# A hybrid attention, state-space and mixture block on one core: passes, sums and a root put at other places

## The chip, the cores and the metric

The kernel runs on one NeuronCore of a Trainium2 chip. TensorE (PE) multiplies, VectorE (DVE), ScalarE (ACT) and GpSimd (POOL) work element by element, and SyncE (SP) issues the transfers. The metric is the device time in microseconds from start to end of one execution. Each engine takes its own instructions strictly in the order in which the program gives them; between engines only semaphores order the work (`wait_ge` holds an engine until a counter is reached, `then_inc` counts up when an instruction is done).

## The reference, cut to what matters

Input is x, 2 batches of 1024 tokens with 128 features, in 32-bit floats. Four blocks follow each other, each on a layer norm of x and each added to x:

```
x = x + attention(layernorm(x))     # 16 heads of 64, causal, values = keys
x = x + ffn(layernorm(x))           # 16 experts of width 64, the best two of 16, and a shared one
x = x + state_space(layernorm(x))   # convolution, gated scan over the tokens
x = x + ffn(layernorm(x))           # the same weights again
```

Attention computes softmax(q k^T / 8) k for each head, masked above the diagonal. Its denominators are sums of exponentials over the keys. The mixture computes for each token `silu(x wg) * (x wu)` for every expert, weights it by the router's share (zero for all but two), and multiplies by wd; it adds the result to the normed input and to x.

## The kernel before, in words

**Attention** (function `attention`, lines 242 to 880) works through 16 units. A unit is a pair of heads (l = 0, 1) of one batch: 1024 queries against 1024 keys, cut by causality into 9 slots of at most 512 query columns for both heads. A slot is a segment of scores for a key block j and query blocks a to b. TensorE fills a pair of PSUM banks with a slot's scores (`scores`, `mask`), ScalarE takes the exponential into SBUF (`exponentials`, L525, one instruction of 128 x 1024 for both heads), TensorE multiplies the keys by it (`outputs`, L783) in five bursts r = 0 to 4. The outputs of a unit run one unit later, beside the next unit's scores; unit 15, the last, has its outputs behind all scores, alone. GpSimd adds the exponentials over the key blocks (`add_up`, L427, 11 sums n = 0 to 10 for each unit; sums 4 to 10 are for the second half of the queries). TensorE then makes a total over partitions (`denominators`, L797), ScalarE the reciprocal (Ln, Exp: L516, L518), and VectorE scales the outputs by it (`scale_out`, L613). The outputs of the first half of a unit's queries lie in the bank `out_ps`, and those of the second half too, except in the last unit, where they lie in a bank of the ring. So outputs of unit 15 may not start before unit 14's second half has been scaled out of `out_ps`:

```
if r == 0:
    pe.wait_ge(knat_done, g + 1)
    wait(pe, out_used, 2 * g)      # g = 15: the 30th scale_out, unit 14, second half
```

VectorE's own order in a unit is: scale the unit before, first half (r = 0), maxima for the unit after, and at r = 4 scale the unit before, second half. In unit 15 there are no maxima to take. GpSimd's wait for a sum is on the exponentials it reads (`exp_done`) and on the sum before.

**The prologue of attention** (L815 to L838) sets up the first two units: TensorE turns the normed input, projects keys and queries, fills banks with scores from which VectorE takes the row maxima (`max_scores(0, m)`, L716; `maxima`, L583 and L587; m = 0 to 9), projects unit 1 (`project`, L680 to L682, 12 passes of 512 columns), turns its keys (`turn_keys(1)`), turns the maxima (`turn_max(0)`, L726) and makes five idle multiplications (`warm`, L808, 128 x 128 in 32-bit floats, two records each in the trace). `warm` exists to keep TensorE at work. The banks of the ring are reused in the written order `PROLOGUE`: m = 8 waits until m = 6 has been read.

**The mixtures** (`mixture`, twice: tags m1 and m2) go through 4 groups of 512 tokens, 9 steps each (8 pairs of experts and the shared one). A step g on TensorE is six passes of 512 columns (`up`, L1047 to L1049: three into a bank g_ps, three into a bank u_ps, both in rings of two) and, two steps later, the down product (`down`, L1058, eight instructions). Between them lie silu on ScalarE (L1142), the weighting on GpSimd (L1280: needs the weights wb, which SyncE spreads by DMA from a tensor in memory), and the product with u_ps on VectorE (L1196, `hid`). A u_ps bank is free for step g when hid of step g - 2 is done. Around the steps, each engine emits the preparation of the groups (source, statistics, root, norm, turn, high and low part, logits, route, turned weights `turn_w`) at due times written out by hand (`PREPARE`, `OWN`, `SOURCE_TILES`): a piece with due time -5 comes before one with -4.5, all with due times below 0 ahead of step 0. In the second mixture the group 0 comes normed from the state-space stage (`first`, early = 1), and the sources of groups 1 to 3 go to g_ps[1], u_ps[0] and u_ps[1].

Of the kernel before, what the change touches and what calls it, by code (L numbers as in the profile page):

```python
# [237 lines left out]
def attention(nc, k, w_qk, x_view, load_w_out):  # L238
# [5 lines left out]
    with Scope(nc, "at") as s:  # L244
# [34 lines left out]
        scores_ready, exp_done, av_done, summed = s.sem("scores_ready"), s.sem("exp_done"), s.sem("av_done"), s.sem("summed_up")  # L279
        den_ready, ln_done, inv_done, out_used = s.sem("den_ready"), s.sem("ln_done"), s.sem("inv_done"), s.sem("out_used")  # L280
        inv_spread = [s.sem(f"inv_spread{h}") for h in range(2)]

# [101 lines left out]
        with nc.Block() as block:  # L384
# [31 lines left out]
            def _(pool):  # L416
                def add_up(unit, n):
# [6 lines left out]
                    wait(pool, summed, NSUM * unit + n)  # L424

                    def add(a, b, left, right):
                        return pool.tensor_tensor(sums[:, :, a * P:b * P], left, right, ALU.add)  # L427

# [139 lines left out]
            def _(dve):  # L568
# [36 lines left out]
                def scale_out(g, half):  # L605
# [3 lines left out]
                    else:  # L609
# [4 lines left out]
                       .then_inc(out_used, 1)  # L614

                clear(dve)
                for n in range(EARLY):
# [24 lines left out]
                for unit in range(UNITS):  # L642
                    more = unit + 1 < UNITS
                    for r, row in rounds(unit):
# [9 lines left out]
                        if r == 0 and unit and more:  # L654
                            keys_low(dve, unit + 1)
                        if r == NBURST - 1:
                            if more:
                                join_maxima(unit + 1)
                            if unit:
                                scale_out(unit - 1, 1)  # L660
                            if more:
                                max_rows(unit + 1)
                            if unit + 2 < UNITS:
                                queries_low(unit + 2)
# [4 lines left out]
            def _(pe):  # L669
# [119 lines left out]
                def denominators(g, half):  # L789

                    pe.wait_ge(summed, NSUM * g + HALF_SUMS[half])
                    if half:
                        pe.wait_ge(rows_done, min(g + 2, UNITS))
# [34 lines left out]
                norm.turn(pe, EARLY + 1)  # L828
                for m in (6, 7, 8):
                    max_scores(0, m)  # L830
                pe.wait_ge(norm.low, GROUPS)
                max_scores(0, 9)
                project(1, "K")
                project(1, "Q")
                turn_keys(1)
                turn_max(0)
                warm(5, out_ps)
# [53 lines left out]
       1: dict(norm=-5.8, residual=-6, turn=-4.5, high=-4, low=-4, natural=1.5, route1=1.6),  # L891
       2: dict(statistics=-4.2, root=-4.1)}
ORDER = ["source", "add_up", "sigmoid"] + [p for p in PREPARE if p != "sigmoid"]


def agenda(pieces, with_finish, tiles=False):

    found = []
    for n in range(GROUPS):
        for piece in pieces:  # L900
# [3 lines left out]
            if piece in PREPARE:  # L904
                at = PREPARE[piece] + STEPS * n
                if piece == "root" and n == 1:
                    at = PREPARE["sigmoid"]
                at = OWN.get(n, {}).get(piece, at)
                found.append((at, piece, n, "prepare"))
# [55 lines left out]
def mixture(nc, tag, k, f, source, source_ready=None, load_x=None, weights=None, next_norm=False, store=None, ahead_of=None, first=None):  # L965
# [9 lines left out]
    with Scope(nc, tag) as s:  # L975
# [12 lines left out]
        before, after = first or GroupNorm(s, "before"), GroupNorm(s, "after") if next_norm else None  # L988
        early = 1 if first else 0

        own = s.ps("own")
# [48 lines left out]
        with nc.Block() as block:  # L1040
            @block.tensor
            def _(pe):
# [20 lines left out]
                def step(g):  # L1063
# [15 lines left out]
                    if g >= RING and (g - RING) % STEPS == LAST:  # L1079
                        pe.wait_ge(hid_ready, g - RING + 1)  # L1080
                    up(g_ps[r], f.wg_hi, f.wg_lo, st, n).then_inc(g_ready, 1)
                    if st < LAST:
                        wait(pe, hid_ready, g - RING + 1)
                        up(u_ps[r], f.wu_hi, f.wu_lo, st, n).then_inc(u_ready, 1)
# [6 lines left out]
                def emit(piece, n, kind):  # L1091
# [27 lines left out]
                    elif piece == "natural":  # L1119
# [6 lines left out]
                        last.then_inc(nat_ready, 1)  # L1126
                    elif piece == "turn_w":
                        pe.wait_ge(w_ready, n + 1)
                        for t in range(PER):
# [767 lines left out]
```

## Time and profile before

| what | us |
|---|---|
| median of the runs (730.75 to 732.27) | 731.11 |
| the profiled execution | 732.0 |
| its span, first to last instruction | 730.1 |
| TensorE busy | 707.1 (97%) |
| VectorE / ScalarE / GpSimd busy | 434.8 / 366.3 / 417.5 |
| mean granted clock of TensorE | 0.989 |

The profiled execution is 0.9 us above the median, and 1.9 us of it lie outside its span. In the page TensorE is at nine tenths or more in nearly all of the 40 slices; it is lower in the first and near 630 us. Its clock is at 0.6 in the second slice (18 to 36 us), and at 0.9 to 1.0 elsewhere. Attention ends at about 452.7 us, the first mixture begins at 453.0, the state-space stage at about 574 and the second mixture at about 626.

### The profile page before, as it was taken

The page shows a single profiled execution, that of the slowest core. Times are in us where ns is not written, and L with a number is a line of the kernel's source. Part 1 is how long each engine was busy: PE and PEld are TensorE (multiplying, and loading weights), DVE is VectorE, ACT ScalarE, POOL GpSimd, SP SyncE. Part 2 cuts the span into 40 slices and gives each one's busy share as a digit, 9 for nine tenths or more (in the row PEclk, how much of TensorE's full clock was granted, in tenths as well). Part 3 has the DMA queues.
Part 4 walks back from the last instruction along what each step waited for, and adds up shares of the span by engine and source line. Part 5 has one row for each costly group of instructions (what it writes and reads, how often), then busy time and mean ns, then how long its engine had stood idle before and what let it go on. Part 6 is the DMA issues. An engine that isn't in the chain of part 4 may idle for free. (4 is left out here: it accounts for less than half of the span.)

```text
span 730.1 us, 14977 instructions
## 1 busy us (share of the span) xinstructions
PE 707.1 (97%) x5675; PEld 499.7 (68%) x5675; DVE 434.8 (60%) x1214; ACT 366.3 (50%) x474; POOL 417.5 (57%) x310
## 2 busy tenths in 40 slices
PE   7899999999999999999999998999999999899998
PEld 6665665666566666566566655988888865678887
DVE  6776766765775775676676511455654657755433
ACT  4465554655555555555465542354664343555421
POOL 4486686677568659659657765144544422354543
PEclk9699999999999999999999999999999999999999
DMA  2000001001001001100100111723223000043332
GB/s 72 8 16 23 26 21 28 24 17 30 24 15 30 23 19 27 29 17 23 27 17 17 31 44 29 177 89 112 97 77 109 1 0 1 6 142 103 105 103 72
DMA packets 41276, 33.49 MB, mean 46 GB/s; under 512 B 14002, under 2 KB 32756, under 8 KB 41204
## 3 DMA queue, kind: packets, MB, share of 16 engines
q1 hardware_dynamic: 41204, 32.52, 15.4%
q8 instruction: 46, 0.75, 0.4%
q14 instruction: 26, 0.21, 0.1%
HBM read 23.32 MB, written 1.31 MB: 34 GB/s over the span
## 5 line engine op out<-in xcount | busy, mean ns | idle before, releaser
L427 POOL TENSOR_TENSOR all_x<-all_x,at_probs 128x1024 f32<-128x1024 f32 (+3 forms) x128 | 208.2, 1627 | 19.0 <-ACT at_probs L525 0.4
L525 ACT ACTIVATE at_probs<-at_ring 128x1024 f32<-128x1024 f32 x144 | 144.3, 1026 | 99.9 <-PE at_ring L762 98.7
L587 DVE CUSTOM_DVE_ANT_0 at_ring<-at_ring,at_after_query 128x128 f32<-128x128 f32 (+3 forms) x252 | 116.9, 516 | 69.1 <-PE at_ring L716 69.1
L783 PE MATMUL at_both<-at_probs,at_k_nat 128*64 128x512 f32 (+1 forms) x736 | 134.3, 493 | 0.2 <-issue 0.2
L1280 POOL TENSOR_TENSOR m_prod<-m_gate,m_wb 128x512 f32<-128x512 f32 x64 | 81.6, 1280 | 87.5 <-ACT m_gate L1142 79.8
L427 POOL TENSOR_TENSOR all_x<-at_probs 128x768 f32<-128x768 f32 (+1 forms) x32 | 67.3, 2102 | 105.1 <-ACT at_probs L525 102.4
L583 DVE TENSOR_REDUCE at_half_max<-at_ring 128x2 f32<-128x1024 f32 x64 | 78.3, 1225 | 42.6 <-PE at_ring L716 42.6
L783 PEld LDWEIGHTS at_both<-at_probs,at_k_nat 128*64 128x64 f32 x736 | 47.0, 136 | 65.3 <-issue 54.5
L1196 DVE TENSOR_TENSOR m_hid<-m_prod,m_u 128x512 f32<-128x512 f32 x64 | 43.7, 686 | 73.5 <-POOL m_prod L1280 70.0
L1058 PEld LDWEIGHTS m_acc<-rest_wd,m_hid 128*128 128x128 f32 (+1 forms) x576 | 74.4, 191 | 7.8 <-DVE m_hid L1196 2.2
L1142 ACT ACTIVATE m_gate<-m_g 128x512 f32<-128x512 f32 (+1 forms) x72 | 42.6, 597 | 70.1 <-PE m_g L1049 68.8
L1058 PE MATMUL m_acc<-rest_wd,m_hid 128*128 128x128 f32 (+1 forms) x576 | 76.1, 276 | 0.0
L716 PE MATMUL at_ring<-at_kh,at_qh 64*128 64x512 f32 (+2 forms) x380 | 71.4, 400 | 2.5 <-DVE at_half_max L583 1.5
L759 PE MATMUL at_ring<-at_qh,at_kl 64*128 64x512 f32 (+3 forms) x384 | 67.1, 343 | 0.0
L753 PE MATMUL at_ring<-at_qh,at_kh 64*128 64x512 f32 (+3 forms) x384 | 66.9, 344 | 0.1
L762 PE MATMUL at_ring<-at_m_rows,at_ones_r 64*128 64x512 f32 (+3 forms) x384 | 66.7, 342 | 0.0
L756 PE MATMUL at_ring<-at_ql,at_kh 64*128 64x512 f32 (+3 forms) x384 | 66.7, 342 | 0.0
L716 PEld LDWEIGHTS at_ring<-at_kh,at_qh 64*128 64x128 f32 x380 | 34.8, 189 | 29.1 <-issue 27.6
L753 PEld LDWEIGHTS at_ring<-at_qh,at_kh 64*128 64x128 f32 x384 | 36.6, 185 | 4.6 <-ACT at_probs L525 0.8
L759 PEld LDWEIGHTS at_ring<-at_qh,at_kl 64*128 64x128 f32 x384 | 36.5, 185 | 4.1
L762 PEld LDWEIGHTS at_ring<-at_m_rows,at_ones_r 64*128 64x128 f32 x384 | 36.6, 185 | 3.8
L756 PEld LDWEIGHTS at_ring<-at_ql,at_kh 64*128 64x128 f32 x384 | 36.3, 185 | 3.8
(254 smaller groups left out, 1189.6 us busy)
## 6 DMA issues: line engine op xcount, KB each, us to landing
m_wb<-m_wt_far SPq DMA_DIRECT2D x128, 128.0 KB, 2.9
at_inv<-at_inv_q SPq DMA_DIRECT2D x240, 32.0 KB, 1.9
all_x<-in_L_attn_a_x SPq DMA_DIRECT2D x8, 256.0 KB, 3.8
at_w_raw<-in_L_attn_a_W_qk SPq DMA_DIRECT2D x8, 128.0 KB, 2.5
out<-all_x SPq DMA_DIRECT2D x4, 256.0 KB, 2.4
a_room<-in_L_attn_a_W_out SPq DMA_DIRECT2D x1, 512.0 KB, 4.2
m_raw_wg<-in_L_ffn_experts_wg SPq DMA_DIRECT2D x1, 512.0 KB, 3.8
m_raw_wu<-in_L_ffn_experts_wu SPq DMA_DIRECT2D x1, 512.0 KB, 3.9
```

Source lines behind the costliest of these rows:

```text
L427: return pool.tensor_tensor(sums[:, :, a * P:b * P], left, right, ALU.add)
L525: act.activation(probs[:, :, slot * BANK:(slot + 1) * BANK], pair("S", unit, slot)[:, :, :], ACT.Exp, scale=BETA).then_inc(exp_done, 1)
L583: last = dve.reduce_max(half_max[:, :, i, out], pair("M", unit, m)[:, :, at:at + w], AX.X)
L587: last = dve.tensor_tensor_reduce(out=sums_ps, in0=sums_ps, in1=after_query[:, BANK - w:BANK], scale=1.0, scalar=MASKED, op0=ALU.add, op1= ...
L716: last = pe.matmul(out[:, l, at:at + (b - a) * P], qh[u][rows(l), i * P:(i + 1) * P], kh[u][rows(l), a * P:b * P], start=True, stop=True)
L753: pe.matmul(to[l], kh[u][rows(l), keys], qh[u][rows(l), q], start=first, stop=False, skip_group_check=True)
L756: pe.matmul(to[l], kh[u][rows(l), keys], ql[u][rows(l), q], start=False, stop=False, skip_group_check=True)
L759: pe.matmul(to[l], kl[u][rows(l), keys], qh[u][rows(l), q], start=False, stop=False, skip_group_check=True)
L762: last = pe.matmul(to[l], ones_r[rows(l), :], m_rows[u][rows(l), q], start=False, stop=True, skip_group_check=True)
L783: last = pe.matmul(out_bank(g, int(r > 0))[rows(l), o:o + (b - a) * P], k_nat[g % 3][:, j, rows(l)], probs[:, l, at:at + (b - a) * P], sta ...
L1058: last = pe.matmul(acc[:, t * P:(t + 1) * P], hid[g % BUFS][h, t * P:(t + 1) * P], f.wd[h, st, :], start=(st == 0 and t == 0), stop=(st == ...
L1280: pool.tensor_tensor(prod[g % BUFS][:, :], gate[g % BUFS][:, :], wb[q % SPREAD][:, :], ALU.mult)\
```

## The change

Four edits.

1. In unit 15 the sums 4 to 10 on GpSimd take head 0 alone (`heads`), and VectorE makes the same sums for head 1 (`last_sums`): the first four at r = 3, the last three at r = 4. The denominators of the second half wait for both.
2. In the prologue TensorE makes eight idle multiplications ahead of `max_scores(0, 8)`, into the bank that the projection of unit 1's keys will use (so they wait for its last reader), and `turn_max(0)` comes before `turn_keys(1)`.
3. In the second mixture the source of group 2 goes into `acc`, and step 0's six passes come ahead of `turn_w` of group 0, behind the sources of group 2, where they followed the turn of group 1.
4. In the second mixture ScalarE's root of group 2 (with the loading of the silu table behind it) comes after the high part of group 1 (due -3.95, where it was -4.1; the high part's is -4).

```diff
@@ add_up (POOL)
+                    heads = slice(0, 1 if unit == UNITS - 1 and n >= HALF_SUMS[0] else 2)
                     def add(a, b, left, right):
-                        return pool.tensor_tensor(sums[:, :, a * P:b * P], left, right, ALU.add)
+                        return pool.tensor_tensor(sums[:, heads, a * P:b * P], left[:, heads, :], right[:, heads, :], ALU.add)
@@ VectorE
+                def last_sums(ns):
+                    g, u = UNITS - 1, sums[:, 1, :]
+                    for n in ns:
+                        slot, seg, a = ((4, 0, 4), (2, 1, 6), (5, 0, 4), (6, 0, 4), (7, 0, 4), (8, 0, 5), (8, 1, 7))[n]
+                        dve.wait_ge(exp_done, NSLOT * g + slot + 1)
+                        if n == 0:
+                            dve.wait_ge(den_ready, dens(g - 1, 2))
+                        wait(dve, last_summed, n)
+                        left = part(3, 0, 4, 8)[:, 1, :] if n == 0 else u[:, a * P:8 * P]
+                        dve.tensor_tensor(u[:, a * P:8 * P], left, part(slot, seg, a, 8)[:, 1, :], ALU.add)\
+                           .then_inc(last_summed, 1)
@@ VectorE's loop over r
                         if r == 0 and unit and more:
                             keys_low(dve, unit + 1)
+                        if r == 3 and not more:
+                            last_sums(range(4))
+                        if r == 4 and not more:
+                            last_sums(range(4, 7))
                         if r == NBURST - 1:
                             if more:
                                 join_maxima(unit + 1)
                             if unit:
                                 scale_out(unit - 1, 1)
@@ denominators (PE)
+                    if half and g == UNITS - 1:
+                        pe.wait_ge(last_summed, 7)
@@ prologue (PE)
-                for m in (6, 7, 8):
-                    max_scores(0, m)
+                max_scores(0, 6)
+                max_scores(0, 7)
+                pair_free(pe, "K", 1)
+                warm(8, pair("K", 1)[:, 0, :])
+                max_scores(0, 8)
                 pe.wait_ge(norm.low, GROUPS)
                 max_scores(0, 9)
                 project(1, "K")
                 project(1, "Q")
+                turn_max(0)
                 turn_keys(1)
-                turn_max(0)
                 warm(5, out_ps)
@@ mixture
-       2: dict(statistics=-4.2, root=-4.1)}
+       2: dict(statistics=-4.2)}
+ROOT_2 = {True: -4.1, False: -3.95}
...
+                if piece == "root" and n == 2:
+                    at = ROOT_2[with_finish]
...
+        if early:
+            src_ps[2] = acc
...
-                    up(g_ps[r], f.wg_hi, f.wg_lo, st, n).then_inc(g_ready, 1)
-                    if st < LAST:
+                    if g or not early:
+                        up(g_ps[r], f.wg_hi, f.wg_lo, st, n).then_inc(g_ready, 1)
+                    if st < LAST and (g or not early):
...
                     elif piece == "turn_w":
+                        if n == 0 and early:
+                            pe.wait_ge(before.low, 1)
+                            up(g_ps[0], f.wg_hi, f.wg_lo, 0, 0).then_inc(g_ready, 1)
+                            up(u_ps[0], f.wu_hi, f.wu_lo, 0, 0).then_inc(u_ready, 1)
                         pe.wait_ge(w_ready, n + 1)
```

## Rows read from the trace of the kernel before

**Rows 1.** The page, busy time by engine: us, share of the span, instructions.

```profile
PE 707.1 (97%) x5675; PEld 499.7 (68%) x5675; DVE 434.8 (60%) x1214; ACT 366.3 (50%) x474; POOL 417.5 (57%) x310
```

**Rows 2.** Waits of TensorE: us in total, times, longest.

```profile
PE m_misc L1115 <- DVE all_xlo L946: 2.4, 2, 1.9
PE m_misc L1130 <- DVE m_w L1249: 2.3, 2, 1.8
```

**Rows 3.** Timeline of TensorE, 442 to 453 us: start, duration, instructions, idle before.

```profile
442.16 2.37 PE L783 MATMUL at_both<-at_probs,at_k_nat 128*64 128x512 f32 x16
444.37 4.03 PE L783 MATMUL at_ring<-at_probs,at_k_nat 128*64 128x512 f32 x20
449.07 1.08 PE L797 MATMUL at_both<-all_x,at_ones 128*64 128x512 f32 x4 [0.67 <-POOL all_x L427]
449.98 1.89 PE L783 MATMUL at_ring<-at_probs,at_k_nat 128*64 128x512 f32 x12
```

**Rows 4.** Timeline of VectorE, 433 to 453 us.

```profile
439.86 0.69 DVE L613 TENSOR_TENSOR a_attn_t<-at_both,at_inv 128x512 f32<-128x512 f32 x1 [15.15 <-PE at_both L783]
...
452.01 0.69 DVE L613 TENSOR_TENSOR a_attn_t<-at_ring,at_inv 128x512 f32<-128x512 f32 x1 [6.64 <-PE at_ring L783]
```

**Rows 5.** Timeline of ScalarE, 440 to 453 us: exponentials of slots 7 and 8.

```profile
441.21 2.12 ACT L525 ACTIVATE at_probs<-at_ring 128x1024 f32<-128x1024 f32 x2 [2.27 <-PE at_ring L762]
```

**Rows 6.** GpSimd, 432 to 453 us: timeline, then groups (busy us, mean ns, idle before).

```profile
437.34 11.67 POOL L427 TENSOR_TENSOR all_x<-all_x,at_probs 128x512 f32<-128x512 f32 x6
...
L427 POOL TENSOR_TENSOR all_x<-all_x,at_probs 128x512 f32<-128x512 f32 x2 | 2.6, 1279 | 0.3
L427 POOL TENSOR_TENSOR all_x<-all_x,at_probs 128x256 f32<-128x256 f32 x2 | 1.5, 726 | 0.3
```

**Rows 7.** Groups of VectorE by shape: busy us, mean ns, idle before.

```profile
L1763 DVE TENSOR_TENSOR m2w_z<-m2w_z,a_attn_t 128x512 f32<-128x512 f32 x2 | 1.3, 682 | 0.0
L1243 DVE TENSOR_TENSOR m_picked<-rest_iota,m_own 128x128 f32<-128x128 f32 x8 | 2.2, 278 | 0.0
```

**Rows 8.** Timeline of TensorE in the prologue, 24 to 35 us.

```profile
25.57 0.80 PE L716 MATMUL at_ring<-at_kh,at_qh 64*128 64x128 f32 x4 [1.48 <-DVE at_half_max L583]
...
26.73 0.79 PE L680 MATMUL at_ring<-all_xhi,at_w_hi 128*128 128x512 f32 x1
...
31.58 0.43 PE L682 MATMUL at_ring<-all_xhi,at_w_lo 128*128 128x512 f32 x1
31.95 0.72 PE L701 MATMUL at_ring<-all_ident,a_room 64*128 64x64 f32 x16
...
32.97 1.38 PE L808 MATMUL at_both<-all_ident 128*128 128x128 f32 x10
34.51 0.29 PE L738 MATMUL at_ring<-at_eye,at_mask 64*128 64x128 bf16 x4 [0.16 <-issue]
```

**Rows 9.** Windows: length, busy of PE, PEld, DVE, ACT, POOL, then PEclk, DMA share, GB/s.

```profile
16.00:18.00 2.00, 0.28 (x2) 0.00 (x0) 1.97 (x12) 0.76 (x2) 2.00 (x3) 1.00 0.00 0
18.00:20.00 2.00, 1.85 (x20) 1.55 (x22) 2.00 (x5) 1.42 (x2) 1.65 (x4) 0.50 0.00 0
...
31.50:34.50 3.00, 2.85 (x32) 2.00 (x31) 1.32 (x2) 2.13 (x4) 2.37 (x1) 0.97 0.00 0
```

**Rows 10.** Timeline of TensorE, 0 to 10 us: the first sixteen idle multiplications.

```profile
1.57 6.78 PE L808 MATMUL at_both<-all_ident 128*128 128x128 f32 x32 [1.57 <-POOL all_ident L354]
```

**Rows 11.** Timeline of VectorE in the prologue: the joining of the maxima.

```profile
29.16 0.19 DVE L596 TENSOR_REDUCE at_row_max<-at_half_max 128x16 f32<-128x32 f32 x1
```

**Rows 12.** Timeline of the second mixture, 641 to 644 us.

```profile
641.32 0.40 PE L1047 MATMUL m_g<-all_xhi,rest_wg_hi 128*128 128x512 f32 x1
...
641.41 1.29 POOL L1280 TENSOR_TENSOR m_prod<-m_gate,m_wb 128x512 f32<-128x512 f32 x1 [4.32 <-DMA m_wb<-m_wt_far]
...
642.74 0.69 DVE L1196 TENSOR_TENSOR m_hid<-m_prod,m_u 128x512 f32<-128x512 f32 x1 [2.18 <-POOL m_prod L1280]
...
643.48 0.51 PE L1047 MATMUL m_u<-all_xhi,rest_wu_hi 128*128 128x512 f32 x1
```

More of the change, by code:

```diff
@@ L280, in attention @@
         den_ready, ln_done, inv_done, out_used = s.sem("den_ready"), s.sem("ln_done"), s.sem("inv_done"), s.sem("out_used")
+        last_summed = s.sem("last_summed")
         inv_spread = [s.sem(f"inv_spread{h}") for h in range(2)]
```

## The prediction

> **What bounds the kernel now.** I read the page's busy times first: TensorE works 97% of the span [rows 1], so it is TensorE's own order that counts. Time is won only where it stands still or runs slowly, and lost wherever a new wait is put in front of it. The list of its waits comes second. It is short; the two of the second mixture are 1.9 us for the low part of group 1 and 1.8 us for the routing weights [rows 2]. I then read timelines of the three places that the diff touches, all engines of each. At the end of attention TensorE waits 0.67 us for GpSimd's sums ahead of the denominators [rows 3]. In the prologue it waits 1.48 us for a maximum [rows 8], and the windows show a granted clock of 0.50 from 18 us on, back at 31.6 or so [rows 9]: that level (1.2 GHz of 2.4) doubles the length of what runs in it.
>
> The sum is made against the profiled execution: 732.0 us, a span of 730.1 and 1.9 around it. It is 0.9 above the median of 731.11; the difference that comes out is then put on the median.
>
> **End of attention: the sums.** GpSimd's six last sums run from 437.34 to 449.01, both heads together [rows 6]. With one head a sum of 1024 becomes one of 512, 1.28 us; one of 384 lies between 0.73 (256) and 1.28, say 1.0; one of 128 is about 0.44 by the same slope [rows 6]. The exponentials of slots 7 and 8 are two of equal kind from 441.21 to 443.33, so slot 7 is there at about 442.3 [rows 5]. GpSimd is then done at 445 to 446, and the wait of 0.67 us [rows 3] goes.
>
> What is late next is the point of this forecast. VectorE's three last sums stand in its order ahead of `scale_out` of unit 14, second half. That instruction runs at 439.86 [rows 4], and TensorE may not begin the outputs of unit 15 before it is done, since both use `out_ps`. Today TensorE comes to this wait at 442.16, 1.6 us after the scaling has ended at 440.55, so the wait costs nothing [rows 3, 4]. After the change the scaling is queued behind sums that need slot 8, at 443.33 [rows 5]. Behind the waiting sum nothing else stands on VectorE, but TensorE waits for that one scaling with all of unit 15's outputs.
>
> Its price needs a VectorE add with both inputs in SBUF: 0.68 us for 512 columns [rows 7], 0.28 for 128 (there one input is in PSUM) [rows 7], so 0.55 for 384. *Lower end*, both engines undisturbed: 443.33 + 0.55 + 0.28 + 0.69 (scaling) + three hand-overs of 0.05 = 445.0, or 2.8 us behind 442.16; less the 0.67 that goes, 2.2 us later. *Upper end*, VectorE's adds and GpSimd's take turns, as GpSimd's first: from 442.3, GpSimd 1.28, VectorE 0.68, GpSimd 1.0, VectorE 0.55, GpSimd 0.44, VectorE 0.28, scaling 0.69, with hand-overs 447.3, or 5.1 behind; less 0.67, 4.5 us. I found no VectorE instruction with two SBUF inputs beside a working GpSimd in this trace; the row of 0.68 was taken while GpSimd stood idle [rows 7]. I take the middle, 3.3 us, because neither end has a row, and keep both. The rest of TensorE's work there, 442.16 to 448.40 and 449.07 to 451.87 [rows 3], moves as a block, and with it the last scaling at 452.01 [rows 4] and the start of the first mixture, which waits for all engines. VectorE's first four sums and the halved sums before them have slack: VectorE was idle for 15 us before 439.86 [rows 4].
>
> One rule speaks on this. The Trainium skill, SBUF — State Buffer, section "Who interferes with whom", says that a VectorE instruction with two SBUF inputs contends with a GpSimd instruction that reads SBUF, and that the later of the two is held for the whole of the other. No run here shows it yet. By it the term would be the upper end, 4.5 us.
>
> **Prologue.** Before: m = 8 and m = 9 take 25.57 to 26.73, twelve passes to 31.98 at about 0.44 each ((31.58 - 26.73) / 11), then the turns and five idle multiplications until 34.35, and unit 0's scores start at 34.51 [rows 8]. At full clock a pass takes 0.24 (nine from 641.32 to 643.48) [rows 12]. The eight added multiplications take 0.42 each at the low rate (sixteen in 6.78 us) [rows 10] or 0.28 at the full one (five in 1.38) [rows 8]: 3.4 or 2.2 us, from 24.1, where 1.48 us were idle. So they push m = 8 back, by 1.9 us at the low rate, and pay only if the clock comes back sooner. It came back 6.0 us after TensorE took up work behind the hole (25.57 to 31.58). Without the hole the unbroken work begins at about 22.6, so I put the return at 28.6: multiplications to 27.5, m = 8 and 9 (1.16) to 28.6, twelve passes at 0.24 to 31.5, and the same 2.4 us to the scores: 33.9, a gain of 0.6 to 0.7 us. The ends: return at the same 31.6, then seven slow and five fast passes from 28.6 to 32.9, a loss of 0.8; return within the first added one, then 2.2 + 0.6 + 2.9 us from 24.1 to 29.8, a gain of 2.3. The order of the turns gives 0.1: the maxima's rows are ready some 0.7 us sooner, but the idle multiplications end last. The join of maxima, now at 29.16 [rows 11], would come at about 31, still before the turn needs it. Sum: -0.7.
>
> **Second mixture.** Six passes (1.4 us) go into the 1.8 us wait for the weights [rows 2]; they were done in front of another wait, so this only shifts idle time. The root behind the high part lets ScalarE do the high part of group 1 some 1.9 us sooner (root, then 1.28 us of table loading, stand before it now), so the 1.9 us wait for the low part [rows 2] goes. But TensorE then runs step 1 and half of step 2 early and stops at step 2's second bank, which needs hid of step 0: VectorE makes it from 642.74 to 643.43, behind GpSimd's product at 641.41, which waited 4.32 us for the weights' DMA [rows 12]. Today TensorE reaches that bank at 643.48 [rows 12], as hid is done. The DMA's chain (route, turned weights, store, spread) is not shortened. So the wait moves and 0.1 us is left (0 to 0.4). Group 2's source in `acc` costs nothing: the first down product comes long after.
>
> **Sum:** 3.3 - 0.7 - 0.1 = +2.5 us: 734.5 in the profiled execution, 733.6 against the median.
>
> **Rivals.**
> *Turns* (taking turns of the two adders, the upper end): 4.5 - 0.8 = +3.7, 734.8. For it: no row of such overlap, and the rule above. Against: as little.
> *Side by side* (lower end): 2.2 - 0.8 = +1.4, 732.5. For it: VectorE with one SBUF input shows the same 0.68 everywhere.
> *The clock falls in the stall.* TensorE stands for 2.8 to 5.1 us. In the prologue the clock went to 0.50 at 18 us after a window with 0.28 us of work in 2 [rows 9], and came back only after 6 us of unbroken work. Six us at half rate cost 3.0: +5.5, 736.6. Against: one hole of 1.9 us [rows 2] left the clock as it was.
> *The warm-up does nothing* for the clock: -0.7 becomes +0.8: 735.1.
> *Not slower:* the clock is back at once in the prologue, worth 2.3 at the place from 24.1 to 34.5, beside the lower end at attention: 2.2 - 2.3 - 0.1 = -0.2, 730.9. It decides from the point where the return comes before some 25 us. Against: six us of nearly full work before 24.1 had not brought it back.
> *The halved sums pay as meant,* the scaling is not in the path: -0.67 - 0.8, 729.6. Only if TensorE's wait for the 30th scaling were not there; the code has it.
>
> **How the numbers follow.** Forecast (around the middle, 732.8 to 734.2) 0.33, turns 0.22, side by side 0.17, clock falls 0.10, warm-up useless 0.07, not slower 0.07, as meant 0.04. The range 731.2 to 736.7 holds all but the last two and the edges. About 0.2% (1.5 us) is what a measurement can tell from no change. Faster (below 729.65): as meant 0.04 and 0.02 of not slower. Within 0.2% (to 732.6): 0.10 of side by side, 0.05 of not slower, 0.07 of the low edges of forecast and warm-up: 0.22. Slower: the rest, 0.72.
>
> **What would show it.** TensorE has a new idle time of 2.8 to 5.1 us before L783 of unit 15, waited for at L613; L613 of unit 14's second half ends after 444.9 and not at 440.55; no wait is left at L797. The new VectorE adds take 0.68 if undisturbed, up to 2 us with GpSimd's turn inside. In the prologue passes of 0.24 begin before 31.6, and scores start before 34.5. In the second mixture the wait at L1115 shrinks and one as long stands at L1047 behind L1196. If TensorE goes into unit 15's outputs without a stop, or the first mixture starts no later than it did, the forecast is wrong.

## The result

The changed kernel takes **737.06 us** (median of 4 runs, 736.65 to 737.4) where the kernel before takes 731.45 beside it (4 runs, 730.75 to 732.27): ratio **1.0078** [1.0066, 1.0091], slower by 5.6 us. The forecast was 733.6, with a range of 731.2 to 736.7: the direction was right, the size too small, and the time lies 0.4 above the range. The two profiled executions differ by less than the medians, since before's was a slow one (732.0 against the median of 731.45) and the change's the fastest of its four. The profiled execution took 736.65 with a span of 734.8, 4.7 more than the 730.1 of before. TensorE is as full as ever, so its work has become longer [rows 1]:

```profile
PE 710.9 (97%) x5691; PEld 503.1 (68%) x5691; DVE 442.5 (60%) x1221; ACT 366.2 (50%) x474; POOL 413.2 (56%) x310
```

Its list of waits (us in total, times, longest) has a new head, and the wait ahead of the denominators is not in it any more. "issue" is a wait that the profile doesn't name a releaser for:

```profile
PE at_both L803 <- issue: 4.2, 2, 4.0
PE m_misc L1148 <- DVE all_xlo L975: 2.2, 2, 1.7
...
PE m_u L1079 <- DVE m_hid L1233: 1.9, 4, 1.0
```

The lines of before that answer to these: L783 is now L803 (outputs), L797 L819 (denominators), L613 L616 (`scale_out`), L427 L430 (GpSimd's sums), L1115 L1148, L1130 L1167, L1047 L1079, L1196 L1233. VectorE's new sums are L629.

**The end of attention.** This timeline of the changed kernel (start, duration, instructions, idle before) answers to [rows 3, 4, 6]. The scaling (L616) stood at 439.86; it is now at 445.57, behind three sums, and TensorE starts unit 15's outputs as it ends:

```profile
442.42 0.69 DVE L629 TENSOR_TENSOR all_x<-all_x,at_probs 128x512 f32<-128x512 f32 x1 [1.83 <-ACT at_probs L528]
442.47 3.63 POOL L430 TENSOR_TENSOR all_x<-all_x,at_probs 128x512 f32<-128x512 f32 x3 [0.72 <-ACT at_probs L528]
443.52 2.13 DVE L629 TENSOR_TENSOR all_x<-all_x,at_probs 128x384 f32<-128x384 f32 x2 [0.40 <-ACT at_probs L528]
445.57 0.68 DVE L616 TENSOR_TENSOR a_attn_t<-at_both,at_inv 128x512 f32<-128x512 f32 x1
...
446.35 3.76 PE L803 MATMUL at_both<-at_probs,at_k_nat 128*64 128x512 f32 x16 [3.96 <-issue]
...
449.84 4.44 PE L803 MATMUL at_ring<-at_probs,at_k_nat 128*64 128x512 f32 x20
...
454.08 1.06 PE L819 MATMUL at_both<-all_x,at_ones 128*64 128x512 f32 x4
...
454.94 1.92 PE L803 MATMUL at_ring<-at_probs,at_k_nat 128*64 128x512 f32 x12
...
457.99 0.68 PE L1899 MATMUL m_g<-a_room,a_attn_t 128*128 128x128 f32 x4 [1.14 <-PEq L385]
```

The first sixteen outputs take 3.76 us where they took 2.37. The windows (length, busy PE, PEld, DVE, ACT, POOL, then PEclk) show why: TensorE's granted clock goes to 0.50, which is 1.2 GHz, some 0.8 us behind the end of the stop (0.79 in the window in which the outputs begin):

```profile
444.00:446.00 2.00, 0.00 (x0) 0.00 (x0) 1.90 (x3) 0.00 (x0) 1.71 (x3) 1.00 0.00 0
446.00:448.00 2.00, 1.65 (x8) 0.78 (x10) 0.25 (x1) 0.00 (x0) 0.10 (x1) 0.79 0.00 0
448.00:450.00 2.00, 2.00 (x14) 1.41 (x12) 0.00 (x0) 0.00 (x0) 0.00 (x0) 0.50 0.00 0
```

Three terms come out. Unit 15's outputs start at 446.35 and not 442.16: 4.19 later. From there to the last group of outputs are 8.59 us, where a kernel with the same sums, but without the stop and the fall of the clock, needs 6.92 (`scale_first` below): 1.67 for the clock. Before, that stretch was 7.82 (442.16 to 449.98), so the wait for GpSimd, gone now, cost 0.90 and not the 0.67 of its row. Sum 4.19 + 1.67 - 0.90 = 4.96: the first mixture's first product stands at 457.99, before at 453.03.

**The prologue** answers to [rows 8, 9]; the clock is back at about 27.3 where it was 31.6, passes of 0.24 start at once, and unit 0's scores begin 1.24 us sooner (34.51 before):

```profile
23.59 3.78 PE L830 MATMUL at_ring<-all_ident 128*128 128x128 f32 x16
...
27.96 0.50 PE L700 MATMUL at_ring<-all_xhi,at_w_hi 128*128 128x512 f32 x1
...
30.61 0.40 PE L702 MATMUL at_ring<-all_xhi,at_w_lo 128*128 128x512 f32 x1
...
33.27 0.28 PE L758 MATMUL at_ring<-at_eye,at_mask 64*128 64x128 bf16 x4
```

The lead is held to unit 15's maxima (419.53, before 420.88) and lost there. Both kernels wait 1.75 us for those maxima; behind that wait the changed one's clock falls, and sixteen outputs take 3.90 us. First the changed kernel:

```profile
419.53 0.44 PE L746 MATMUL at_both<-all_ident,at_row_max 128*64 128x128 f32 x4 [1.75 <-DVE at_row_max L599]
420.17 3.90 PE L803 MATMUL at_both<-at_probs,at_k_nat 128*64 128x512 f32 x16 [0.20 <-issue]
```

and the same place before:

```profile
420.88 0.44 PE L726 MATMUL at_both<-all_ident,at_row_max 128*64 128x128 f32 x4 [1.75 <-DVE at_row_max L596]
421.53 2.37 PE L783 MATMUL at_both<-at_probs,at_k_nat 128*64 128x512 f32 x16 [0.20 <-issue]
```

3.90 - 2.37 = 1.53 is lost, and the changed kernel is then 0.16 behind. So the last sums themselves cost 4.96 - 0.16 = 4.8.

**The second mixture** answers to [rows 12]. The wait for the weights (L1167) has shrunk to 0.41, and a wait of 1.02 stands at step 2's second bank, behind `hid`:

```profile
639.47 0.60 PE L1167 MATMUL m_misc<-all_ident,m_w 128*16 128x128 f32 x4 [0.41 <-DVE m_w L1286]
644.01 0.39 PE L1148 MATMUL m_misc<-all_xhi,rest_gate_hi 128*16 128x512 f32 x1 [1.71 <-DVE all_xlo L975]
...
647.98 0.50 PE L1079 MATMUL m_u<-all_xhi,rest_wu_hi 128*128 128x512 f32 x1 [1.02 <-DVE m_hid L1233]
```

GpSimd's product there waited 3.82 us for the weights' transfer. From the second mixture's first source to the end are 103.75 us (631.05 to 734.8), before 104.0 (626.08 to 730.1): -0.3. The three parts give 4.8 + 0.2 - 0.3 = 4.7, the difference of the spans.

### The profile page after: what moved, and what is told of

The parts are those of the page before. It is cut to its first block and busy times, and to the rows that moved or that the text cites. A ratio compares the mean times of both kernels' runs of the same rounds, so it can differ in the third digit from the quotient of the medians.

```text
span 734.8 us, 15024 instructions
## 1 busy us (share of the span) xinstructions
PE 710.9 (97%) x5691; PEld 503.1 (68%) x5691; DVE 442.5 (60%) x1221; ACT 366.2 (50%) x474; POOL 413.2 (56%) x310
## 5 line engine op out<-in xcount | busy, mean ns | idle before, releaser
L430 POOL TENSOR_TENSOR all_x<-all_x,at_probs 128x1024 f32<-128x1024 f32 (+4 forms) x128 | 204.7, 1599 | 20.3 <-ACT at_probs L528 2.0
L803 PE MATMUL at_both<-at_probs,at_k_nat 128*64 128x512 f32 (+1 forms) x736 | 137.2, 502 | 4.2 <-issue 4.2
L430 POOL TENSOR_TENSOR all_x<-at_probs 128x768 f32<-128x768 f32 (+2 forms) x32 | 66.5, 2077 | 105.1 <-ACT at_probs L528 102.5
L803 PEld LDWEIGHTS at_both<-at_probs,at_k_nat 128*64 128x64 f32 x736 | 48.2, 139 | 70.8 <-issue 60.1
L1233 DVE TENSOR_TENSOR m_hid<-m_prod,m_u 128x512 f32<-128x512 f32 x64 | 43.8, 687 | 74.9 <-POOL m_prod L1317 71.5
L1179 ACT ACTIVATE m_gate<-m_g 128x512 f32<-128x512 f32 (+1 forms) x72 | 42.6, 597 | 70.1 <-PE m_g L1081 68.8
```

What stands on the lines that cost most here:

```text
L430: return pool.tensor_tensor(sums[:, heads, a * P:b * P], left[:, heads, :], right[:, heads, :], ALU.add)
L803: last = pe.matmul(out_bank(g, int(r > 0))[rows(l), o:o + (b - a) * P], k_nat[g % 3][:, j, rows(l)], probs[:, l, at:at + (b - a) * P], sta ...
```

## The experiments

Each part alone came first, then the change with one thing altered. The edits are shown shortened. "Change" is the changed kernel. All ratios are against the kernel before on the same chip.

**only_sums: the new sums alone**

```
- prologue and second mixture as before
+ GpSimd: heads 0 only for n > 3 of unit 15;  VectorE: last_sums(range(0, 4)), last_sums(range(4, 7))
```

> The kernel before with the change of attention's last sums alone. Theory (the scaling of unit 14's second half is queued on VectorE behind the last three sums, these take turns with GpSimd's, and the stop of TensorE lets its clock fall): the changed kernel's trace shows TensorE's outputs of unit 15 begin 4.0 us late and attention end 5.0 us later, so +5 to +6.5 us here, all or more of what the whole change costs. Rival (the loss lies elsewhere, for example in falls of the clock that the new prologue's timing brings about): +2 us or less here.

735.4 us (735.03 to 736.99), ratio 1.0058 [1.0045, 1.0071]. Its timeline of TensorE:

```profile
444.54 3.40 PE L803 MATMUL at_both<-at_probs,at_k_nat 128*64 128x512 f32 x16 [3.97 <-issue]
...
453.13 1.92 PE L803 MATMUL at_ring<-at_probs,at_k_nat 128*64 128x512 f32 x12
```

The stop is 3.97, and 444.54 to 453.13 are 8.59 us, as in the change. The first mixture begins 3.16 us later than in before's profile (456.19 to 453.03), though unit 0's scores began 1.66 sooner (32.85): 4.8 for the sums, as in the change. So the larger part of the loss lies here, though the median is only 3.8 us above the kernel before and not the 5 to 6.5 expected.

**only_prologue: the prologue's edits alone**

```
-for m in (6, 7, 8): max_scores(0, m)
+max_scores(0, 6); max_scores(0, 7)
+pair_free(pe, "K", 1); warm(8, pair("K", 1)[:, 0, :]); max_scores(0, 8)
... (turn_max(0) after the two statistics' turns -> before them)
```

> The kernel before with the prologue's edits alone (eight idle multiplications ahead of m = 8, turn of maxima first). Theory: the trace of the changed kernel has the scores of unit 0 start 1.24 us sooner and the lead kept for 14 units, so -1.2 us (-0.6 to -1.4). Rival: the lead is paid back by a fall of the clock in a later unit, as in that trace at 420 us, so 0 (-0.3 to +0.5).

732.51 us (729.68 to 734.12, 12 runs), ratio 1.0001 [0.9988, 1.0013]: nothing. The runs lie in two groups, up to 731.3 and from 732.48 on (7 runs), the upper with a mean clock of 0.988 against 0.993 to 0.995. The profiled one is the highest, and its windows show two places at 1.2 GHz:

```profile
422.00:424.00 2.00, 2.00 (x8) 0.70 (x6) 0.00 (x0) 0.00 (x0) 1.86 (x2) 0.50 0.00 0
...
636.00:638.00 2.00, 2.00 (x11) 2.00 (x11) 1.97 (x8) 0.59 (x1) 1.23 (x1) 0.50 0.11 24
```

The second lies behind the 1.79 us wait for the routing weights of the second mixture, most of which the mixture's edit takes away (0.41 is left in the change).

**only_mixture: the second mixture's edits alone**

```
+ group 0: step 0's six passes ahead of the turned weights; root of group 2's statistics at -3.95; src_ps[2] = acc
```

> The kernel before with the second mixture's edits alone (first passes early, source in acc, root later). Theory (the wait moves from the low part of group 1 to the hid of step 0): -0.1 to -0.4 us, and in the trace a wait of about 1.0 us at the u passes of step 2 behind hid. Rival (the wait of 1.9 us is won): -1.5 to -1.9 us.

730.75 us (729.84 to 731.38), ratio 0.9988 [0.9979, 0.9997]. The list of waits from 625 to 655 us has the wait at its new place:

```profile
PE m_misc L1139 <- DVE all_xlo L966: 2.2, 2, 1.7
PE m_u L1070 <- DVE m_hid L1224: 0.9, 1, 0.9
```

A gain of 0.12% is 0.9 us (0.2 to 1.5), more than the 0.1 us forecast. In the profile the stretch from the second mixture's first source to the end is shorter by only 0.2 (103.8 against 104.0). The rest may be falls of the clock behind the 1.8 us wait for the weights, which this edit shortens to 0.4: such a fall stands in the profiles of only_prologue and before_filled, which have the old mixture. That it is the rest of the gain is not shown.

The three parts do not add up in the medians: 0.58% + 0.01% - 0.12% is 0.47%, and the change has 0.78%. The change's profile has a fall of the clock at 420 us that the profile of only_sums lacks, and all four of its runs have the same mean clock, 0.988; that all four fall there is likely, not shown.

**scale_first: is it the order on VectorE?** The change with the last three sums behind the scaling:

```
 scale_out(14, 0)
-last_sums(range(4, 7)); scale_out(14, 1)
+scale_out(14, 1); last_sums(range(4, 7))
```

> The changed kernel with one thing moved: VectorE scales unit 14's second half ahead of its last three sums, not behind them. Theory: the stop of 4.0 us ahead of unit 15's outputs and the fall of the clock in it are gone, and the wait of 0.67 us for the sums too: -0.7 - 1.2 - 0.3 = 2.2 us faster than the kernel before (1 to 2.5), 7 to 8 faster than the changed kernel. Rival (VectorE and GpSimd taking turns, not the order, is what costs): the sums still end late, and the time stays within 1 us of the kernel before or above it.

730.63 us (728.25 to 734.73, 11 runs), ratio 0.9988 [0.9974, 1.0002]; the profiled execution 728.32. Timeline of VectorE, GpSimd and TensorE:

```profile
437.87 0.68 DVE L616 TENSOR_TENSOR a_attn_t<-at_both,at_inv 128x512 f32<-128x512 f32 x1
439.68 2.38 PE L803 MATMUL at_both<-at_probs,at_k_nat 128*64 128x512 f32 x16
439.78 0.69 DVE L629 TENSOR_TENSOR all_x<-all_x,at_probs 128x512 f32<-128x512 f32 x1 [1.23 <-ACT at_probs L528]
439.82 3.66 POOL L430 TENSOR_TENSOR all_x<-all_x,at_probs 128x512 f32<-128x512 f32 x3 [0.73 <-ACT at_probs L528]
440.87 2.15 DVE L629 TENSOR_TENSOR all_x<-all_x,at_probs 128x384 f32<-128x384 f32 x2 [0.40 <-ACT at_probs L528]
...
445.75 1.03 PE L819 MATMUL at_both<-all_x,at_ones 128*64 128x512 f32 x4
446.60 1.89 PE L803 MATMUL at_ring<-at_probs,at_k_nat 128*64 128x512 f32 x12
```

No stop, no wait before the denominators, no clock fall. By the ratio the gain is 0.9 us and not the 2.2 expected, and its interval reaches 1; the profiled run is one of the three fastest. The adders take turns as before (2.15 us for two adds), and that costs nothing, since only the denominators at 445.75 need them. So the order is the cause, and with it put right the halved sums pay 0.9 us at this place. The medians do not show that gain (without_sums below has 0.9989, this kernel 0.9988), since most runs here lie in an upper group; its three lowest (728.25 to 728.59) are 0.4 to 1.4 below the seven lowest of without_sums (729.02 to 729.68).

**pool_silent: how much of the stop is the turns?** The change, and GpSimd leaves out its last three sums of unit 15 (head 0's totals lack those slots).

```
-for n in range(NSUM):
+for n in range(NSUM if unit < UNITS - 1 else 8):
```

> The changed kernel, but GpSimd leaves out its sums 8, 9 and 10 of unit 15 (head 0's denominators of its second half lack slots 7 and 8), so that VectorE's last three adds run with GpSimd idle. Theory (the adds of the two engines take turns): VectorE's three adds take 0.68, 0.55 and 0.28 us, the scaling ends at 445.0 to 445.2 on the changed kernel's time scale and not at 446.25, TensorE stands 2.8 us and not 4.0, so at least 1.2 us faster than the changed kernel; if the clock then holds, 2.9. Rival (VectorE's adds are slow by themselves, two SBUF inputs and a semaphore each): the adds take as long as in the changed kernel, 2.1 us for the last two, and the stop stays 4.0.

734.41 us (734.01 to 735.76), ratio 1.0048 [1.0033, 1.0062]. Timeline of VectorE and TensorE, then windows:

```profile
440.02 0.69 DVE L629 TENSOR_TENSOR all_x<-all_x,at_probs 128x512 f32<-128x512 f32 x1 [1.83 <-ACT at_probs L528]
441.12 0.95 DVE L629 TENSOR_TENSOR all_x<-all_x,at_probs 128x384 f32<-128x384 f32 x2 [0.40 <-ACT at_probs L528]
441.99 0.68 DVE L616 TENSOR_TENSOR a_attn_t<-at_both,at_inv 128x512 f32<-128x512 f32 x1
442.78 4.53 PE L803 MATMUL at_both<-at_probs,at_k_nat 128*64 128x512 f32 x16 [2.78 <-issue]
...
452.66 1.90 PE L803 MATMUL at_ring<-at_probs,at_k_nat 128*64 128x512 f32 x12
```

```profile
442.00:444.00 2.00, 1.22 (x4) 0.59 (x6) 0.67 (x2) 0.00 (x0) 0.00 (x0) 0.50 0.00 0
...
446.00:448.00 2.00, 2.00 (x13) 1.08 (x12) 0.58 (x1) 0.00 (x0) 0.00 (x0) 0.50 0.00 0
```

Two adds take 0.95 us beside a silent GpSimd, 2.13 beside a working one, and the stop is 2.78, the forecast's lower end. But the clock stays at 1.2 GHz for some 7 us here, and outputs to last outputs take 9.88: 2.96 for the clock, 1.29 more than in the change, against 1.18 saved in the stop. At this place nothing is won; its lower time goes with a quicker prologue (scores at 32.38, not 33.27) and no fall at 420 us.

**warm_stall: what is the clock fall worth?** The change with idle multiplications in the stop:

```
+if g == UNITS - 1:
+    pe.wait_ge(ln_done, 2 * g + 1); warm(12, misc)
 ... (TensorE's wait for the scaling of unit 14, then outputs of unit 15)
```

> The changed kernel, with twelve idle multiplications of TensorE in the stop ahead of unit 15's outputs. Theory: they fill about 3 of the 4.0 us, the clock does not fall there, and the outputs' first 36 records take 6.2 us as before and not 7.7: 1.5 to 1.7 us faster than the changed kernel, with the scaling still late. Rival (the outputs are slow for another reason, such as memory access beside the adders): no change.

733.56 us (731.97 to 735.54, 10 runs), ratio 1.0028 [1.0017, 1.0039]. Timeline of TensorE:

```profile
442.95 2.94 PE L833 MATMUL at_both<-all_ident 128*128 128x128 f32 x24
446.95 2.37 PE L806 MATMUL at_both<-at_probs,at_k_nat 128*64 128x512 f32 x16 [1.05 <-DVE a_attn_t L616]
...
453.88 1.89 PE L806 MATMUL at_ring<-at_probs,at_k_nat 128*64 128x512 f32 x12
```

The stop is as long, but 446.95 to 453.88 are 6.93 us and the clock stays at 2.4 GHz: all of the 1.67 comes back. The median is 3.5 us below the change's and not 1.7: this profiled execution, the highest, has the fall at 420 us and is 1.1 below the change's, but half of the runs lie in a second group at 731.97 to 732.66. Those were not profiled; that they lack the fall is likely, not shown.

**without_sums: the rest of the change**

```
- GpSimd and VectorE share unit 15's sums
+ GpSimd makes them alone, as before (prologue and second mixture as in the change)
```

> The changed kernel with the sums of attention as before: prologue and mixture edits together. If the edits simply add up: only the prologue 0 (730.0 to 732.5 in two groups by the mean clock) and only the mixture -0.9, so -0.9 us against before in the median, in two groups, 729 and 732; the rival, that the mixture's edit fills the second hole in which the clock fell in the prologue kernel's trace, gives a smaller upper group and -1.5 us.

729.67 us (729.02 to 731.84, 12 runs), ratio 0.9989 [0.9978, 0.9999]. Seven runs lie at 729.02 to 729.68, five at 731.43 to 731.84. Prologue and mixture do pay. The upper five have a mean clock of 0.991, the lower seven 0.992 to 0.995, which speaks for a fall of the clock that takes the gain back; only a run of the lower group was profiled (729.05, no fall at 420 us).

**filled: scale_first and a filled hole at 420 us**

```
+if r == 0 and unit == UNITS - 1:
+    pair_free(pe, "S", unit, 0); warm(7, pair("S", unit, 0)[:, 0, :])
 turn_max(unit)
```

> The kernel with the scaling put first, and seven idle multiplications in the 1.75 us in which TensorE waits for unit 15's maxima. Theory (the spread of the kernels with the new prologue comes from falls of the clock at about 420 us, seen in two traces, in that hole): no fall there, the group of runs at 730.5 goes and the median is 728.3 to 729, 2.5 to 3.3 below before. Rival (the falls are elsewhere, or come at random anywhere): spread and median as in the kernel without the filling, 730.6.

**728.39 us** (728.33 to 728.9, 5 runs), ratio 0.9963 [0.995, 0.9975]. Timeline of TensorE; the wait of 1.75 is now full of work, and the outputs take 2.38, as in the executions without a fall:

```profile
416.71 1.83 PE L830 MATMUL at_ring<-all_ident 128*128 128x128 f32 x14
418.53 0.44 PE L746 MATMUL at_both<-all_ident,at_row_max 128*64 128x128 f32 x4
419.17 2.38 PE L803 MATMUL at_both<-at_probs,at_k_nat 128*64 128x512 f32 x16 [0.20 <-issue]
```

What speaks for the filling is the spread: eight of the eleven runs of scale_first lie at 730.31 or above, and none of these five.

**without_sums_filled and before_filled: the same filling elsewhere**

```
(the same three lines, in without_sums and in the kernel before)
```

> Prologue and mixture edits, attention's sums as before, and the seven idle multiplications in the 1.75 us ahead of unit 15's maxima. Theory (that hole makes the upper of the two groups): one group of runs at 729.0 to 729.7, median 729.2; the difference to the kernel with the scaling put first and the same filling (728.4) is what the halved sums are worth in the right order, 0.67 us by the wait. Rival (the groups come from elsewhere): still some runs at 731.5.

> The kernel before with the seven idle multiplications alone. If the clock falls at 420 us in the kernel before too, it gets faster by some 0.5 to 1.5 us in the median; if it never falls there in it (the runs of before lie within 1.7 us of each other), nothing changes: 731.3.

without_sums_filled: 730.13 us (728.84 to 730.8, 11 runs), 0.9981 [0.9971, 0.999]. The group above 731.4 is gone, but the lower one, around 729.3, has not come back: nine runs lie at 729.8 to 730.8. The profiled one had a late clock in the prologue (scores at 33.66, not 32.04); whether that holds for the nine is not shown. before_filled: 731.74 (11 runs), 1.0 [0.9991, 1.0009]: no gain. That fits the four profiled executions with the old prologue and this hole open, none of which falls there. The profile of before_filled does have a fall elsewhere: behind the 1.79 us wait for the second mixture's weights, where sixteen multiplications take 3.58 us and not 1.95.

**mixture_no_dma: does the weights' transfer set the moved wait?** only_mixture, and step 0 of group 0 multiplies `gate` by itself and not by the weights (they are left out there).

```
-pool.wait_ge(wb_loaded[q % SPREAD], ...); tensor_tensor(prod, gate, wb[q % SPREAD])
+if not (early and q == 0): pool.wait_ge(...)
+if early and q == 1: pool.wait_ge(wb_loaded[0], 32)      # step 1 waits for both transfers
+tensor_tensor(prod, gate, gate if early and q == 0 else wb[q % SPREAD])
```

> The kernel with the mixture's edits alone, in which GpSimd multiplies the gate of step 0 of group 0 by itself, in place of the spread weights, so that this step waits for no DMA (the weighting of that one step is left out). Theory (the DMA's chain holds hid of step 0, and with it the u passes of step 2): the wait of 0.9 us at these passes goes, and the kernel is 0.9 us faster than the one with the mixture's edits (730.75), 729.8. Rival (the wait has another cause, such as the silu with its table): no change.

730.79 us (729.73 to 731.69, 10 runs), 0.9991 [0.9982, 1.0001], as only_mixture. Timeline of VectorE, ScalarE, GpSimd and TensorE:

```profile
640.95 0.69 DVE L1224 TENSOR_TENSOR m_hid<-m_prod,m_u 128x512 f32<-128x512 f32 x1 [2.43 <-POOL m_prod L1311]
...
641.70 0.50 PE L1070 MATMUL m_u<-all_xhi,rest_wu_hi 128*128 128x512 f32 x1
641.81 1.28 ACT L1170 ACT_TABLE_LOAD   x1
643.11 1.09 ACT L1170 ACTIVATE m_gate<-m_g 128x512 f32<-128x512 f32 x2
...
643.78 3.75 POOL L1311 TENSOR_TENSOR m_prod<-m_gate,m_wb 128x512 f32<-128x512 f32 x3 [2.86 <-DMA m_wb<-m_wt_far]
...
645.84 0.50 PE L1070 MATMUL m_u<-all_xhi,rest_wu_hi 128*128 128x512 f32 x1 [1.04 <-DVE m_hid L1224]
```

At step 2 the wait is gone (641.70), so the transfer did set it; but one of 1.04 us stands one step on, and the time is the same. By its times this second one is set by ScalarE and not by the transfer, though the row names the transfer. GpSimd's product of step 1 starts at 643.78, 0.07 us behind the end of the first of the two silu instructions (643.11, 0.60 us), and that one stood behind the table load (641.81, 1.28). The last packets for step 1's weights are counted at 643.13, 0.6 earlier. In the change, too, the row of this product names ScalarE (649.01, idle for 1.80 until the silu of L1179). So the rival of this run, the silu with its table, is what limits next.

**filled_again**: the kernel of filled once more.

> The kernel with the scaling put first and the hole ahead of unit 15's maxima filled, timed a second time, since the same filling did not lower the median of the kernel without the halved sums. If 728.4 was typical, again 728.3 to 728.9 in every run. If those five runs were all from the lucky side of the clock's return in the prologue, a median of 729 to 729.5 with runs up to 730.2; the upper group of the unfilled kernel (730.3 to 731.4) stays away in either case.

728.58 us (728.04 to 729.97, 8 runs), 0.9971 [0.9961, 0.9982]. Three runs lie at 729.6 to 729.97, so the narrow spread of the first five was in part luck. It is the best version: 2.1 to 2.7 us below the kernel before, about 8 below the change.

Across the profiled executions, from the same rows of each: start of unit 0's scores; start of the turn of unit 15's maxima behind the hole at 420 us, and whether the clock fell there; start of unit 15's outputs to the last group of them; start of the first mixture, us.

| kernel | scores | hole at 420 | outputs | mixture | us |
|---|---|---|---|---|---|
| before | 34.51 | 420.88, no | 7.82 (0.90 of it a wait) | 453.03 | 732.0 |
| change | 33.27 | 419.53, yes | 8.59 | 457.99 | 736.65 |
| only_sums | 32.85 | 419.24, no | 8.59 | 456.19 | 735.4 |
| only_prologue | 33.95 | 420.18, yes | 7.79 | 453.95 | 734.12 |
| only_mixture | 32.91 | 419.30, no | 7.79 | 451.43 | 730.14 |
| mixture_no_dma | 34.29 | 420.69, no | 7.78 | 452.79 | 731.5 |
| pool_silent | 32.38 | 418.65, no | 9.88 | 455.71 | 734.35 |
| warm_stall | 33.81 | 420.08, yes | 6.93 | 456.94 | 735.54 |
| scale_first | 32.13 | 418.40, no | 6.92 | 449.66 | 728.32 |
| without_sums | 32.04 | 418.26, no | 7.81 | 450.39 | 729.05 |
| filled | 32.32 | filled | 6.92 | 449.79 | 728.39 |
| filled_again | 31.96 | filled | 6.93 | 449.41 | 728.04 |
| without_sums_filled | 33.66 | filled | 7.79 | 452.03 | 730.67 |
| before_filled | 32.77 | filled | 7.77 | 451.26 | 731.64 |

## Why the prediction was off

- **The stop before unit 15's outputs: right.** Forecast 2.8 to 5.1, the middle 3.95 (3.3 + 0.67); measured 3.96. L616 ends at 446.25, "after 444.9". That it is the order on VectorE is shown by scale_first. That the middle held is luck, since no row spoke for it: the adders did take turns, but VectorE, not GpSimd, went first (442.42 against 442.47), and of the six adds taken in turns, VectorE's last ended at 445.65, before GpSimd's last (446.10). The lower end is shown too, 2.78, with GpSimd silent.
- **The rule on two SBUF inputs: right as a mechanism, and only a part of the stop.** VectorE's last two adds take 2.13 us and 2.15 beside GpSimd's, 0.95 without them. The Trainium skill, SBUF — State Buffer, "Who interferes with whom", says that a VectorE instruction with two SBUF inputs contends with a GpSimd instruction that reads SBUF; the trace agrees. The turns add 1.18 us to the stop, not the 2.3 between my ends, which assumed that GpSimd went first.
- **The clock in the stop: the step that failed.** I made it a rival with a chance of 0.10, arguing that one hole of 1.9 us had left the clock as it was, though the stop forecast was twice as long. All three profiles with an unfilled stop (change, only_sums, pool_silent) show the fall, and warm_stall, with the stop filled, does not. It costs 1.67, 1.67 and 2.96 us, where I priced 3.0. It belonged into the sum. The one hole was no argument either: holes of 1.75 to 1.79 us were followed by a fall in four profiles (change, warm_stall and only_prologue at 420 us, only_prologue and before_filled in the second mixture).
- **The wait for GpSimd: gone as forecast,** worth 0.90 and not 0.67, since idle time counts only from the modelled end of the multiplications before it: without a wait the denominators start ahead of that end (scale_first: 445.75, the end being 441.88 + 4.03 = 445.91). The last sums: forecast +3.3, measured 4.8; of the 1.5 between, the clock is 1.67, the larger wait -0.2.
- **Prologue: the mechanism right, the term wrong for the whole run, and the second step that failed.** Forecast: return of the clock at 28.6, scores at 33.9, -0.7. Measured: 27.3, 33.27, -1.24. What I did not foresee is that it is paid back at 420 us: +1.53, from a hole that had no fall in the kernel before. In only_prologue the net over the runs is nothing. Nor is -1.24 a clean number: scores began between 32.77 and 34.51 in five profiles with the old prologue, between 31.96 and 33.95 in nine with the new one. The means are 33.47 and 32.84, 0.6 apart, as forecast. The profile of before that I read was the latest of its five, which flattered the gain. The rival of a clock that is back at once came near in five of the nine, where it was back by 25.5 us. One row was misread: the 0.42 us of one idle multiplication [rows 10] I called the low rate, but the windows of before give a clock of 1.00 from 0 to 8 us; at 0.50 the eight added ones took 3.78 us, 0.47 each.
- **Second mixture: right that the wait moves, too small in the runs.** The wait moved from the weights (1.8, now 0.41) to step 2's second bank behind L1233 (1.02); -0.3 in the profiles, -0.12% [-0.21, -0.03] or -0.9 us when timed alone, forecast -0.1. "The 1.9 us wait for the low part goes" was wrong: it is 1.71, since TensorE comes to it sooner as well. The chain of the transfer, which the forecast named, sets the place at step 2; with it out of the way ScalarE's silu behind its table load sets the next, and nothing is won (mixture_no_dma).
- **The range** gave +5.5 for the clock's fall as an upper end, with nothing behind it. 737.06 has the stop, the clock, and no net gain from the prologue, three terms that I never added up together. From the forecast of +2.5 to the 4.7 between the profiles: +1.7 for the clock, +0.9 for the prologue (+0.2 net at the end of attention and not -0.7), -0.2 for the larger wait, -0.2 for the mixture. The medians are another 0.9 apart, because I put a difference against one profiled execution, a high one, on the median.

**Open.** Why the hole at 420 us, 1.75 us in all ten profiles that have it open, makes the clock fall in three. The prologue as such is not what tells them apart: change, warm_stall, pool_silent and scale_first have the same instructions up to there, and two fall. The place in time does: the three falls are those in which TensorE starts again at 419.53 to 420.18 us of the span; none is among the seven at 418.26 to 419.30 and at 420.69 to 420.88, where the executions with the old prologue happened to lie. Three falls are too few to show that this is the cause. One run of scale_first at 734.73 was not profiled. Why most runs of without_sums_filled lie above the lower group of without_sums; in the one profiled, the later scores (33.66 against 32.04) make up the whole 1.62 us.

## What to carry to other kernels

Work given to an idle engine is cheap only if nothing that the busiest engine needs stands behind it in that engine's order: look for the next instruction behind each added one, and put it first (the other order took the kernel from 1.0078 to 0.9988 [0.9974, 1.0002]). A stop of TensorE is priced as its length and the slow clock behind it, here 1.7 to 3.0 us for a stop of 2.8 to 4 us; fill a stop that can't be removed with idle multiplications. Where the same kernel's runs form two groups, compare their mean clocks and look for one hole behind which it falls.

## What the runs showed of the hardware

- The shorter stop had the longer slow clock: 2.78 us, then some 6.8 at 1.2 GHz and 2.96 lost (pool_silent, one profile); 3.96 and 3.97, then some 3.4 at 1.2 GHz and 1.67 lost (change, only_sums). Shortening the stop without filling it won nothing at its place.
- A hole of 1.75 us was followed by a clock of 1.2 GHz in some executions (change, warm_stall) and not in others with the same instructions up to there (scale_first, pool_silent). One of 1.79 us was followed by it in before_filled and not in before.
- With the same instructions up to there, the clock's return in the prologue lay between 25.0 and 28.2 us in the nine profiles with the new prologue and between 29.0 and 31.7 in the five with the old one; the scores moved by up to 2.0 and 1.7 us.
